# Ternary jobs moved in TensorE's order, and the keys-values and query operands moved in SBUF, in a fused attention and FFN kernel

## What is computed

```python
q, k, v = split(xn @ Wqkv + bqkv); qp = elu(q) + 1; kp = elu(k) + 1
kv = einsum('bsd,bse->bde', kp, v); num = einsum('bsd,bde->bse', qp, kv)
den = einsum('bsd,bd->bs', qp, kp.sum(axis=1))
z = layer_norm(xn + num / (den + 1e-6)) * g1 + b1
ffn = (silu(z @ Wg + bg) * (z @ Wu + bu)) @ Wd + bd      # hidden width 682
s = layer_norm(z + ffn) * g2 + b2
tern = clip(round(W / mean|W|), -1, 1)
out = x + s * silu(xn @ (tern * mean|W|).T)
```

## Time and profile before

| | us |
|---|---|
| median of 3 runs (lowest, highest) | 1210.75 (1208.73, 1210.92) |
| profiled execution | 1209.84 |
| its span, first to last instruction | 1208.1 |
| PE busy | 1187.2 (98%) |
| DVE busy | 1079.5 (89%) |
| ACT busy | 953.2 (79%), 148.8 of it in 116 table loads |
| POOL busy | 843.7 (70%) |

### The profile page before, as it was taken

How to read it: one execution, slowest core, us unless ns; L and a number is a source line. 1 busy time by engine, 2 the same in 40 slices (tenths; PEclk the granted TensorE clock), 3 DMA queues, 4 the chain that set the end, 5 groups by cost and what they waited for, 6 DMA issues and landing times.

```text
span 1208.1 us, 24021 instructions
## 1 busy us (share of the span) xinstructions
PE 1187.2 (98%) x7550; PEld 1067.3 (88%) x7550; DVE 1079.5 (89%) x2467; ACT 953.2 (79%) x1557; POOL 843.7 (70%) x994
## 2 busy tenths in 40 slices
PE   8999999999999999999999999999999999999997
PEld 6889998989988999988989989899988999888886
DVE  6988999999999999999999999999999999777765
ACT  7787888878888888888878888788887878867753
POOL 3443787767787776787757887677886767766676
PEclk9999999999999999999999999999999999999999
DMA  7213432334432334432334432244332343222201
GB/s 216 78 48 88 123 106 70 88 106 123 123 104 72 88 106 123 122 105 73 88 106 122 110 103 83 75 123 123 109 96 67 97 123 105 71 71 63 76 21 36
DMA packets 137523, 115.61 MB, mean 96 GB/s; under 512 B 12339, under 2 KB 122293, under 8 KB 137398
## 3 DMA queue, kind: packets, MB, share of 16 engines
q1 hardware_dynamic: 137398, 114.08, 32.6%
HBM read 67.38 MB, written 46.67 MB: 94 GB/s over the span
## 4 chain that ended last, share of the span: by engine, by line
PE 52%; DVE 21%; ACT 11%; issue 9%; DMA 3%; POOL 2%; SPq 1%; DVEq 0%; ACTq 0%; POOLq 0%
PE bank L1271 36%; PE d_bank L1271 11%; PE xk_bank L1271 5%; DVE st L922 3%; DVE bank L1095 3%; ACT rz L695 3%; DVE rz L1054 2%; DVE h_l L1105 2%; DMA xa<-z_turned 2%; DMA z_turned<-xa 2%; ACT h_h L695 1%; DVE zT_l L1085 1%; ACT ku L695 1%; POOL norm L569 1%; ACT hs L695 1%
## 5 line engine op out<-in xcount | busy, mean ns | idle before, releaser
L1271 PE MATMUL bank<-zT_h,wgu_h 128*128 128x512 f32 x704 | 275.1, 391 | 1.1 <-DVE rz L1054 1.1
L1271 PE MATMUL bank<-zT_l,wgu_h 128*128 128x512 f32 x704 | 275.1, 391 | 0.0
L1271 PE MATMUL bank<-zT_h,wgu_l 128*128 128x512 f32 x704 | 275.0, 391 | 0.0
L695 ACT ACTIVATE rz<-rz,norm 128x256 f32<-128x256 f32 x252 | 140.5, 595 | 53.6 <-DVE norm L1131 53.6
L569 POOL TENSOR_TENSOR norm<-ve,consts 128x4 f32<-128x4 f32 x64 | 72.9, 1139 | 154.7 <-DVE ve L933 154.5
L1271 PE MATMUL d_bank<-wd_h,h_h 128*128 128x256 f32 x640 | 179.4, 280 | 0.1
L1271 PE MATMUL d_bank<-wd_h,h_l 128*128 128x256 f32 x640 | 179.2, 280 | 0.0
L1271 PE MATMUL d_bank<-wd_l,h_h 128*128 128x256 f32 x640 | 179.2, 280 | 0.0
L1095 DVE SCALAR_TENSOR_TENSOR bank<-bank,hb,hs 128x512 f32<-128x512 f32 x160 | 117.9, 754 | 53.6 <-ACT hs L695 41.9
L695 ACT ACTIVATE h_h<-bank 128x512 fp32r<-128x512 f32 x160 | 95.7, 598 | 80.7 <-DVE bank L1095 80.4
L1271 PEld LDWEIGHTS bank<-zT_l,wgu_h 128*128 128x128 f32 x704 | 132.2, 188 | 28.1
(11 more groups left out here) (163 smaller groups left out, 3571.8 us busy)
## 6 DMA issues: line engine op xcount, KB each, us to landing
xq<-in_L_attn_x_dram SPq DMA_DIRECT2D x32, 512.0 KB, 5.9
xa<-in_L_attn_x_dram SPq DMA_DIRECT2D x31, 512.0 KB, 3.9
out_dram<-rz SPq DMA_DIRECT2D x31, 512.0 KB, 5.0
z_turned<-xa SPq DMA_DIRECT2D x120, 128.0 KB, 3.3
xa<-z_turned SPq DMA_DIRECT2D x30, 512.0 KB, 4.1
turned<-xa SPq DMA_DIRECT2D x108, 128.0 KB, 2.4
xa<-turned SPq DMA_DIRECT2D x27, 512.0 KB, 3.9
rz<-in_L_attn_Wg_dram SPq DMA_DIRECT2D x1, 640.0 KB, 5.7
```

Of the source, the lines that this page charges most:

```text
L695: return eng.activation(out_, in_, func, **kw).then_inc(S[name], 1)
L1271: ins = eng.matmul(dst, left, right, start=first and n == 0, stop=last and n == len(pairs) - 1, **kw)
```

## The change

It moves both ternary jobs in TensorE's order: B 0 from ahead of U 2 to behind Q 1, ahead of G 3; B 1 from ahead of G 3 to behind U 4, ahead of XK 1. On ScalarE silu_tern 0 goes from behind h_high 1 to the place between q_high 0 and q_high 1, where silu_tern 1 was, and silu_tern 1 goes behind h_high 3. The lists of VectorE, GpSimd and SP stay. In SBUF, `SHIFT` goes, `kv_h` and `kv_l` become four tensors `kv_h0`, `kv_h1`, `kv_l0`, `kv_l1` between the down weights and the query weights, with small tensors between them, and `xk_copy` and `xk_low` work in two halves of 256 columns instead of one step of 512.

```diff
--- before.py
+++ after.py
@@ -49,7 +49,6 @@
 LEAD = GPB + 1
 PLAIN = GPB
 KVW = D + 2
-SHIFT = 8
 LN_EPS = 1e-5
 ATTN_EPS = 1e-6
 SCALE_EPS = 1e-5
@@ -88,14 +87,14 @@
 LATE_D = 4
 TENSOR_JOBS = steps("""
-    K 0, D 4, KV 0, KV 1, D 5, K 1, N 0, N 1, N 2, N 3, G 0, U 0, G 1, U 1, G 2, B 0, U 2, Q 0, Q 1,
-    B 1, G 3, D 0, D 1, U 3, G 4, XK 0, U 4, XK 1, XK 2, XK 3, GU 5, D 2, TZ 0, TZ 1, D 3""")
+    K 0, D 4, KV 0, KV 1, D 5, K 1, N 0, N 1, N 2, N 3, G 0, U 0, G 1, U 1, G 2, U 2, Q 0, Q 1,
+    B 0, G 3, D 0, D 1, U 3, G 4, XK 0, U 4, B 1, XK 1, XK 2, XK 3, GU 5, D 2, TZ 0, TZ 1, D 3""")
 SCALAR_STEPS = steps("""
     xk_copy 0, zT_high 0, zT_high 1, x_res 0, x_res 1, kv_high 0, kv_high 1, x_res 2, x_res 3, k_exp 0,
-    last_rows 0, silu_gate 0, h_high 0, silu_gate 1, last_rows 1, h_high 1, silu_tern 0, last_rows 2,
-    silu_gate 2, last_rows 3, k_exp 1, k_high 0, q_exp 0, h_high 2, z_rows 0, z_rows 1, z_rows 2,
-    z_rows 3, q_exp 1, k_high 1, q_high 0, silu_tern 1, q_high 1, silu_gate 3, silu_gate 4, x_high 0,
-    h_high 3, x_high 1, h_high 4, silu_gate 5, xn_high 0, xn_high 1, h_high 5""")
+    last_rows 0, silu_gate 0, h_high 0, silu_gate 1, last_rows 1, h_high 1, last_rows 2, silu_gate 2,
+    last_rows 3, k_exp 1, k_high 0, q_exp 0, h_high 2, z_rows 0, z_rows 1, z_rows 2, z_rows 3, q_exp 1,
+    k_high 1, q_high 0, silu_tern 0, q_high 1, silu_gate 3, silu_gate 4, x_high 0, h_high 3, silu_tern
+    1, x_high 1, h_high 4, silu_gate 5, xn_high 0, xn_high 1, h_high 5""")
 VECTOR_STEPS = steps("""
     xk_low 0, zT_low 0, k_add 0, zT_low 1, kv_bias 0, kv_bias 1, kv_low 0, kv_low 1, ffn_rows 0,
     ffn_rows 1, k_add 1, last_stats 0, attn 0, last_shift 0, attn 1, attn 2, attn 3, h_rows 0, k_max 0,
@@ -230,8 +229,6 @@
         NGU = (2 * HF + 1) * P
-        hb = sb("hb", [P, 2 * HC])
-        rstd0 = sb("rstd0", [P, LN0, TILES])
         wk_h = sb("wk_h", [P, DC, D], f32r)
         wk_l = sb("wk_l", [P, DC, D], f32r)
         tern = sb("tern", [P, DC, D], f32r)
@@ -239,7 +236,21 @@
         kp_l = sb("kp_l", [P, TILES, D], f32r)
         wd_h = sb("wd_h", [P, HC, D], f32r)
         wd_l = sb("wd_l", [P, HF, D], f32r)
+        kv_h0 = sb("kv_h0", [P, KVW], f32r)
+        rstd0 = sb("rstd0", [P, LN0, TILES])
+        hb = sb("hb", [P, 2 * HC])
         hb0 = sb("hb0", [P, 2 * HC])
+        kv_h1 = sb("kv_h1", [P, KVW], f32r)
+        nmr0 = sb("nmr0", [P, LN0, TILES])
+        hb1 = sb("hb1", [P, 2 * HC])
+        ve = sb("ve", [P, 3, TILES])
+        kv_l0 = sb("kv_l0", [P, KVW], f32r)
+        mv = sb("mv", [P, 3, TILES, 2])
+        vecs = sb("vecs", [P, 5, DC])
+        consts = sb("consts", [P, 4])
+        masks = sb("masks", [P, 2])
+        kv_l1 = sb("kv_l1", [P, KVW], f32r)
+        norm1 = sb("norm1", [P, 2, TILES])
         wq_h = sb("wq_h", [P, DC, D], f32r)
         wq_l = sb("wq_l", [P, DC, D], f32r)
         xT_h = sb("xT_h", [P, XT, DC, TOK], f32r)
@@ -253,20 +264,10 @@
         xn_l = sb("xn_l", [P, TILES, D], f32r)
         wgu_h = sb("wgu_h", [P, DC, NGU], f32r)
         wgu_l = sb("wgu_l", [P, DC, NGU], f32r)
-        qp_h = sb("qp_h", [P, DC, TOK + SHIFT], f32r)
-        consts = sb("consts", [P, 4])
-        nmr0 = sb("nmr0", [P, LN0, TILES])
-        kv_h = sb("kv_h", [P, DC, D + SHIFT], f32r)
-        qp_l = sb("qp_l", [P, DC, TOK + SHIFT], f32r)
-        masks = sb("masks", [P, 2])
-        mv = sb("mv", [P, 3, TILES, 2])
-        kv_l = sb("kv_l", [P, DC, D + SHIFT], f32r)
-        norm1 = sb("norm1", [P, 2, TILES])
+        qp_h = sb("qp_h", [P, DC, TOK], f32r)
+        qp_l = sb("qp_l", [P, DC, TOK], f32r)
         norm2 = sb("norm2", [P, 2, TILES])
         den = sb("den", [P, 2, 2])
-        hb1 = sb("hb1", [P, 2 * HC])
-        ve = sb("ve", [P, 3, TILES])
-        vecs = sb("vecs", [P, 5, DC])
         tscale = sb("tscale", [P, 4])
         st = sb("st", [P, 3, TILES, 6])
         ident = sb("ident", [P, P])
@@ -287,6 +288,7 @@
         rz = sb("rz", [P, RZ, TILES, D])
         sg = sb("sg", [P, SG, TILES, D])
         hs = sb("hs", [P, 2, TOK])
+        kv_h, kv_l = (kv_h0, kv_h1), (kv_l0, kv_l1)
         ones, one_zero, neg_half = consts[:, 0:1], consts[:, 1:3], consts[:, 3:4]
         bq, bq1, nbq, g1c, b1c = (vecs[:, n, :] for n in range(5))
         less_h, less_w = masks[:, 0:1], masks[:, 1:2]
@@ -386,7 +388,7 @@
         block = ctx.enter_context(nc.Block())
-        xk_h, xk_l = kv_h[:, :, 0:D], kv_l[:, :, 0:D]
+        xk_h, xk_l = [kv_h[c][:, 0:D] for c in range(DC)], [kv_l[c][:, 0:D] for c in range(DC)]
         raw_v = xq[:, 1:3, :, :].rearrange("p a t d -> p (a t d)")[:, NGU:NGU + DC * D].rearrange("p (c n) -> p c n", c=DC)
         raw_qk = qp
@@ -845,13 +847,14 @@
                     eng.wait_ge(S["XK"], TILES * (g + GPB))
                     if g:
                         eng.wait_ge(S["N"], TILES * g)
-                    act(xk_h, xk_bank[:, :].rearrange("p (c n) -> p c n", c=DC), ACT.Copy, "xk")
+                    for c in range(DC):
+                        act(xk_h[c], xk_bank[:, c * D:(c + 1) * D], ACT.Copy, "xk")
             def kv_high(g, c):
                 if g % GPB == 0:
                     eng.wait_ge(S["kv"], DC * (g // GPB) + c + 1)
                     eng.wait_ge(S["KV"], DC * (g // GPB + 1))
-                    act(kv_h[:, c, 0:KVW], job_bank("KV", g, c)[:, 0:KVW], ACT.Copy, "kvh")
+                    act(kv_h[c][:, 0:KVW], job_bank("KV", g, c)[:, 0:KVW], ACT.Copy, "kvh")
             def silu_tern(g, p):
                 eng.wait_ge(S["B"], PAIRS * g + p + 1)
@@ -1150,9 +1153,10 @@
             def xk_low(g, _=0):
                 if g % GPB == 0:
-                    eng.wait_ge(S["xk"], g // GPB + 1)
-                    eng.tensor_tensor(xk_l, xk_bank[:, :].rearrange("p (c n) -> p c n", c=DC),
-                                      xk_h.bitcast(f32), ALU.subtract).then_inc(S["xkl"], 1)
+                    eng.wait_ge(S["xk"], DC * (g // GPB + 1))
+                    for c in range(DC):
+                        eng.tensor_tensor(xk_l[c], xk_bank[:, c * D:(c + 1) * D], xk_h[c].bitcast(f32),
+                                          ALU.subtract).then_inc(S["xkl"], 1)
             def setup_v_low():
                 eng.wait_ge(S["w_vh"], 1)
...
@@ -1345,14 +1349,14 @@
             def KV(g, c, dst):
                 batch = g // GPB
-                eng.wait_ge(S["xkl"], batch + 1)
+                eng.wait_ge(S["xkl"], DC * (batch + 1))
                 eng.wait_ge(S["ks"], TILES * (g + GPB))
                 if g == 0:
                     eng.wait_ge(S["w_vl"], 1)
                 w = slice(c * P, (c + 1) * P)
                 products(dst[:, 0:D], [
                     pair for k in range(DC)
-                    for pair in parts3(xk_h[:, k, w], xk_l[:, k, w], wv_h[:, k, :], wv_l[:, k, :])], None)
+                    for pair in parts3(xk_h[k][:, w], xk_l[k][:, w], wv_h[:, k, :], wv_l[:, k, :])], None)
                 products(dst[:, D:KVW], [(ksum[:, batch % 2, w], one_zero[:, :])], "KV")
             def N(g, t, dst):
@@ -1361,7 +1365,7 @@
                 s = slice(t * P, (t + 1) * P)
                 products(dst[:, 0:KVW], [
                     pair for c in range(DC)
-                    for pair in parts3(qp_h[:, c, s], qp_l[:, c, s], kv_h[:, c, 0:KVW], kv_l[:, c, 0:KVW])], "N")
+                    for pair in parts3(qp_h[:, c, s], qp_l[:, c, s], kv_h[c][:, 0:KVW], kv_l[c][:, 0:KVW])], "N")
             def gate_or_up(g, at, dst, name):
                 eng.wait_ge(S["zTl"], PAIRS * (g + 1))
```

More of the change, by code:

```diff
@@ L1171, in kv_low @@
                     eng.wait_ge(S["kvh"], DC * (g // GPB) + c + 1)
-                    eng.tensor_tensor(kv_l[:, c, 0:KVW], job_bank("KV", g, c)[:, 0:KVW],
-                                      kv_h[:, c, 0:KVW].bitcast(f32), ALU.subtract).then_inc(S["kvl"], 1)
+                    eng.tensor_tensor(kv_l[c][:, 0:KVW], job_bank("KV", g, c)[:, 0:KVW],
+                                      kv_h[c][:, 0:KVW].bitcast(f32), ALU.subtract).then_inc(S["kvl"], 1)
             def setup_bk():
@@ L1334, in XK @@
                 if n == 0:
-                    eng.wait_ge(S["xkl"], g // GPB)
+                    eng.wait_ge(S["xkl"], DC * (g // GPB))
                 for c in range(DC):
```

## The result

The changed kernel takes 1217.82 us (median of 4 runs, 1217.22 to 1218.86) against 1209.82 us (4 runs) on the same chip: ratio 1.0071, 95% interval 1.0059 to 1.0084, or 8 us slower. Forecast were 1223 us and slower, in a range of 1211 to 1229. The profiled execution took 1218.86 us, its span 1217.1 us.

What follows compares the result with a forecast made beforehand. TensorE (98% busy) bounds the kernel, VectorE's queue nearly as long. 19 x 0.52 + 6 x 0.66 = 13.8 us, less 1.1, gives +12.7 on 1209.84: 1222.5, plus 0.9 for the median: 1223 us; range 1211 to 1229.

Steps and rivals of the forecast that it cites:

- Two loops of nearly one length, and the lead of 0.94 us runs into VectorE's queue: TensorE and VectorE's queue nearly tie; TensorE jobs wanted 0.94 us earlier meet unchanged VectorE steps, G 4 stalling 0.52 us.
- 19 x 0.52: Term for iterations 1 to 25 without a batch boundary: 19 iterations, each with a 0.52 us stall at G 4.
- 6 x 0.66: Term for the six iterations with xk_copy and xk_low: 0.66 us stall each, halved copies adding 0.14 us.
- G 4 starts 0.05 us behind q_elu 0: Expected sign on TensorE: G 4 waits directly for VectorE's q_elu 0, giving a GU 5 to GU 5 period of 36.2 us.
- U 3 ... up to 0.2 us late, but G 4 behind it is later still, so this adds nothing: On TensorE, U 3 waits for VectorE's h_low 2 up to 0.2 us, at no cost beyond G 4's wait.
- the hold: VectorE's k_low 0 taking 1.23 instead of 0.67 us, 0.56 us, by GpSimd contention; assumed paid once in each iteration.
- the sum stays: While GpSimd is dense, VectorE's lost time moves from step to step, but its total per iteration is unchanged.
- B 1 in time by 0.1 us: On TensorE, B 1 is wanted at 570.78, and ScalarE's silu_tern 0 ends at 570.6, so no wait.
- partly absorbed: Rival: the hold on k_low goes in some iterations, 0.1 to 0.3 us each instead of 0.52: 1213 to 1218; chance 0.13.
- the third rival: B 1 is late too: ScalarE loses 0.6 us, B 1 waits 0.45 us more per iteration: 1234 us; chance 0.08.
- the placement: New SBUF addresses: N gains at most 1.0 us by the rows, zero by the skill; taken as 0.
- The ends at zero, and 1.1 us off for zT_low: Iterations 0 and 26 to 30 add zero; half of zT_low's 2.3 us of DMA waits goes, 1.1 us off.

Runs made afterwards that it cites:

- the placement alone: The kernel before with the changed layout and the copies and subtractions in halves, its job lists kept: 1208.70 us, ratio 0.9999.
- B 0 put back: The changed kernel with B 0 and silu_tern 0 returned to their old places, B 1 staying behind U 4: 1205.96 us, ratio 0.9978 to the kernel before.
- B 1 alone: The kernel before, layout and all, with only B 1 moved behind U 4 and silu_tern 1 behind h_high 3: 1206.79 us, ratio 0.9982.
- B 0 alone: The kernel before, layout and all, with only B 0 and silu_tern 0 moved, B 0 to just ahead of B 1: 1328.84 us, ratio 1.0990.

## Why the prediction was right, and where not

- *Two loops of nearly one length, and the lead of 0.94 us runs into VectorE's queue*: right. The change is slower because of it, and the mean plain period of 36.21 us is the 36.2 forecast. But it was forecast on top of iteration 13's 35.68, and the mean before was 35.84, as some iterations had waits of their own that the reorder removed. So the term "19 x 0.52" should have been 19 x 0.37 = 7.0 us, and that the period came out at 36.2 us is luck: the base was 0.16 us too low and the stall 0.15 us too high. The six boundary iterations, "6 x 0.66", measured 0.63. Together 10.8 instead of 13.8 us.
- *"G 4 starts 0.05 us behind q_elu 0"*: wrong, G 4 starts 0.30 us behind it and U 3 pays, 11 us in all. The step that failed is "U 3 ... up to 0.2 us late, but G 4 behind it is later still, so this adds nothing". It placed the hold between h_low 2 and q_elu 0 (in k_low 0). In the changed kernel it falls on k_max 1, ahead of h_low 2, or on neither, and then U 3's wait already gives the queue all it needs. The hold was named as the open quantity; its place was not followed through to who would wait. Nor does "the sum stays" hold: in 11 of the 19 plain iterations VectorE does not pay the hold at all, and its stretch is 26.72 us, where the forecast had 27.33 us in every one.
- *"B 1 in time by 0.1 us"*: wrong by little. silu_tern 0 ended 32.97 us after GU 5 in iteration 13 (576.71 - 543.74), and the forecast had 32.96 (570.6 - 537.64). TensorE was there earlier than forecast, 32.76 instead of 33.14 us after GU 5: 0.3 us of it by its own products, as the last point tells, the rest because U 3 held it up by less than 0.52 us. So B 1 waits 0.26 us wherever VectorE's stretch is short. The two waits together keep the period between 36.08 and 36.44 us: VectorE's queue sets one, ScalarE's the other.
- *The rivals and the signs*: all three signs that the prediction gave for being wrong are there (a queue well under 27.3 us, G 4 over 0.1 us behind q_elu 0, a wait of B 1). The time, 1217.8 us, lies below the forecast's own 1219 to 1229 and in the range of the rival "partly absorbed" (1213 to 1218, given 0.13). That the hold goes in some iterations, as that rival says, is what the rows show, only that B 1 (the third rival, given 0.08) then waits and takes back a part of it. Slower, and the range of 1211 to 1229, held.
- *"U 2, Q 0 and Q 1 show no wait"* and *"the placement"* at 0: right. The rule of the Trainium skill (TensorE: Matmul & The Clock Gate, "Step-by-step: what each phase is for") that loading weights takes no read bandwidth from the running matmul agrees with it: by it the placement gives zero, and the placement alone measured 0.9999.
- *Which of the two is held*: the trace agrees in part with the Trainium skill (SBUF — State Buffer, "Who interferes with whom"), by which the order of issue decides which of the two instructions is blocked. In iteration 13 before, k_low 0 (565.57, 1.23 us) started 0.07 us behind the GpSimd step below and was held. But in the two pairs of rows in "What GpSimd adds", VectorE's step starts first by about 0.02 us both times, and once GpSimd and once VectorE is held, so those rows do not show what decided.

```profile
565.50 0.74 POOL L615 TENSOR_TENSOR rz<-rz,sg 128x256 f32<-128x256 f32 x1
```

- *The ends at zero, and 1.1 us off for zT_low*: nearly. The head and the tail together are 1.75 us shorter than before, and the listed waits of zT_low fell from 2.3 to 0.4 us.
- *What was not in the sum*: TensorE's own products. K 0's twelve, and the first product behind them, before and after:

```profile
541.83 0.28 PE L1271 MATMUL bank<-wk_h,xT_h 128*128 128x256 f32 x1
...
543.25 0.28 PE L1271 MATMUL d_bank<-wd_h,h_h 128*128 128x256 f32 x1
```

```profile
547.87 0.28 PE L1275 MATMUL bank<-wk_h,xT_h 128*128 128x256 f32 x1
...
549.23 0.28 PE L1275 MATMUL d_bank<-wd_h,h_h 128*128 128x256 f32 x1
```

1.42 against 1.36 us. The +10.8 us of the 25 iterations are made up of 11.2 and 3.8 us more of waits at U 3 and B 1 and 4.7 us by which the products behind these waits come more slowly, less 3.4 us at the Q jobs (their waits of before) and 5.5 us at D, K and XK (0.7 us of it waits of K 0 before). Over iterations 1 to 29 the runs of D, K and XK give back about 4.4 us in the changed kernel against a start-to-start time of 117.2 ns, and about nothing before. That lets TensorE arrive 0.3 us earlier at U 3, where it waits. It would also explain why B 0 put back and B 1 alone are faster than before while their listed waits are not shorter: there D and K give back some 4 us, and the Q jobs take 1.3 us of it. That this is their gain is argued from the timeline, not shown by a run.

## What to carry to other kernels

Before moving a job past others, list for each job whose buffer it takes afterwards, not only how much work lies ahead of it: one place in a ring of five banks decided here between 0.2% faster and 10% slower. Where the busiest engine leads by a few tenths of a microsecond, removing the first wait uncovers the next one on another engine, so work the slack of each waiter out from the mean over iterations and not from one. If a step's duration varies, follow each of its possible places in the queue to the job that would wait.

## What the runs showed of the hardware

**Two rhythms of products.** Runs of 256-column products with new weights each go at 113 to 114 ns from start to start or at 117 to 118 ns, within one kernel and at the same granted clock of 1.00. The weight load then starts 110 or 114 to 115 ns ahead of its product. A run keeps its rhythm over K, D 4, D 5 and K 1. In the changed kernel iteration 13 goes over to the fast one in D 0, behind G 3 with uneven starts, and in B 1 behind the wait. What starts it was not settled.

**What a wait of 3 us does to the clock.** B 0 alone, iteration 14; windows with the busy us (instructions) of PE, PEld, DVE, ACT, POOL and then the granted clock, and G 3 to D 0 in the timeline:

```profile
661.00:665.00 4.00, 0.97 (x8) 0.76 (x8) 4.00 (x8) 3.97 (x8) 3.92 (x6) 1.00 0.18 34
665.00:668.00 3.00, 3.00 (x12) 2.57 (x13) 2.83 (x4) 2.96 (x6) 3.00 (x4) 0.63 0.58 129
```

```profile
664.84 0.50 PE L1271 MATMUL bank<-zT_h,wgu_h 128*128 128x512 f32 x1 [3.03 <-DVE h_l L1105]
...
665.95 0.63 PE L1271 MATMUL bank<-zT_h,wgu_l 128*128 128x512 f32 x1
666.37 0.63 PE L1271 MATMUL bank<-zT_l,wgu_h 128*128 128x512 f32 x1
666.80 0.41 PE L1271 MATMUL d_bank<-wd_h,h_h 128*128 128x256 f32 x1
667.01 0.42 PE L1271 MATMUL d_bank<-wd_h,h_l 128*128 128x256 f32 x1
```

Here TensorE restarts at full speed after an idle time of 3 us and 1.1 us later falls to 1.2 GHz: 0.42 us from one 512-column product to the next instead of 0.23, 0.21 instead of 0.12 for 256 columns, for some 3 us. It is not the same behind each of these waits: in 15 of the 25 iterations the granted clock falls 0.4 to 1.4 us after G 3 restarts, in iterations 3, 7 and 15 it has fallen 1 us before that restart and stays down for 6.8 us, and in the other seven (4, 10, 12, 17, 19, 22 and 24) it stays at full speed although the waits are about as long. In the two jobs behind the wait, the products take about 33 us too long over the kernel (12 us in the G jobs, 21 us in D), which with the 86 us of listed waits for h_l over the whole execution makes the 120 us. The waits of 0.3 to 0.9 us in the changed kernel did not do this: its granted clock is 0.998, as before.
